# A graph network on one core: Q rows brought into PSUM by a transpose in place of a product with the identity

## The reference

```python
h   = x @ W1 + b1
e   = concatenate([h[dst], h[src] - h[dst]], axis=-1)
m   = relu(e @ W2 + b2)
m   = relu(m @ W3 + b3)
out = relu(segment_max(m, dst, num_segments=N))     # then x = layernorm(x + out)
```

## Time and profile before

| | |
|---|---|
| median of 3 runs | 7734.12 us (7720.88 to 7736.13) |
| profiled execution, its own time | 7735.87 us |
| its span in the trace | 7734.6 us |
| mean granted TensorE clock | 0.794 of full speed |
| PE busy, share of the span | 5133.2 us, 66% |
| PEld | 3121.7 us, 40% |
| DVE | 3723.3 us, 48% |
| ACT | 2423.4 us, 31% |
| POOL | 4559.1 us, 59% |

### The profile page before, as it was taken

The page is one execution under the profiler, slowest core; times in us unless marked ns, Lnnn a source line. Parts: engine busy times, 40 slices in busy tenths (PEclk is TensorE's granted clock), DMA queues, the critical chain, the costliest instruction groups (busy, mean ns, idle before and its releaser), DMA issues.

```text
span 7734.6 us, 94535 instructions
## 1 busy us (share of the span) xinstructions
PE 5133.2 (66%) x25906; PEld 3121.7 (40%) x25906; DVE 3723.3 (48%) x10623; ACT 2423.4 (31%) x7395; POOL 4559.1 (59%) x4719
## 2 busy tenths in 40 slices
PE   3467777777777266767777777725777767767771
PEld 2355555555556133333333333312333333333330
DVE  2222222222223355656666656535665656655664
ACT  1111111111112333333333333323433433333343
POOL 5666666666665655555555555555555555555553
PEclk6787788877788588888888888857888888888885
DMA  4566666666666233333333333313333333333332
GB/s 111 143 183 177 180 182 178 182 180 183 177 182 174 54 85 89 91 88 89 91 90 89 91 85 91 88 48 83 92 89 88 91 84 93 87 89 87 88 92 61
DMA packets 779198, 875.08 MB, mean 113 GB/s; under 512 B 128800, under 2 KB 609525, under 8 KB 778670
## 3 DMA queue, kind: packets, MB, share of 16 engines
q0 software_dynamic: 150304, 304.49, 18.0%
q1 hardware_dynamic: 365790, 354.92, 14.1%
q10 hardware_dynamic: 262576, 209.63, 10.6%
HBM read 536.77 MB, written 331.81 MB: 112 GB/s over the span
## 4 chain that ended last, share of the span: by engine, by line
PE 58%; issue 28%; DVE 4%; another core or an unknown queue 4%; SPq 3%; ACT 2%; POOL 0%; DMA 0%; ACTq 0%; DVEq 0%; POOLq 0%
PE ps L1199 40%; PE ps L1142 5%; PE ps L1132 4%; PE ps L1131 4%; PE ps L1152 3%; SPq L298 1%; SPq L295 1%; DVE ring_b L938 1%; DVE ring_a L892 0%; DVE ring_a L899 0%; POOL ring_a L407 0%; PE ps L1177 0%; ACT x_sb L555 0%; ACT work L509 0%
## 5 line engine op out<-in xcount | busy, mean ns | idle before, releaser
L440 POOL DMA_INDIRECT ring_a<-H_table,src_i x2784 | 2675.5, 961 | 2042.4 <-DVE ring_b L938 1248.4
L1199 PE MATMUL ps<-work,ring_a 128*128 128x390 bf16 x9576 | 1930.8, 359 | 548.0 <-issue 514.4
L1199 PE MATMUL ps<-work,ring_b 128*128 128x390 bf16 x7182 | 1490.6, 345 | 845.9 <-issue 842.0
L380 POOL DMA_INDIRECT ring_a<-Q_table,src_i x1563 | 1513.9, 969 | 827.9 <-issue 455.9
L1199 PEld LDWEIGHTS ps<-work,ring_a 128*128 128x128 bf16 x9576 | 991.1, 105 | 1519.4 <-issue 985.1
L892 DVE TENSOR_TENSOR ring_a<-code,ps 128x896 bf16<-128x896 int16 x1368 | 843.0, 616 | 1279.4 <-remote 1071.9
L590 ACT ACTIVATE code<-src_row,code_bias 128x128 int16<-128x128 int32 x2052 | 636.7, 388 | 2609.5 <-DVE ring_b L892 2562.5
L1199 PEld LDWEIGHTS ps<-work,ring_b 128*128 128x128 bf16 x7182 | 709.3, 100 | 1510.7 <-issue 1091.3
L807 DVE TENSOR_TENSOR_SCAN work<-tab_flat,work,ps 128x512 f32<-128x512 bf16 x390 | 498.8, 1279 | 1607.8 <-remote 1300.7
L938 DVE SCALAR_TENSOR_TENSOR ring_b<-ring_b,gc,ring_a 128x129 f32<-128x129 f32 x3124 | 1092.7, 350 | 138.4 <-issue 66.0
L604 ACT ACTIVATE ring_a<-ring_a,ge 128x129 f32<-128x129 f32 x3126 | 954.9, 390 | 11.4
(11 more groups left out here) (236 smaller groups left out, 2265.8 us busy)
## 6 DMA issues: line engine op xcount, KB each, us to landing
run_sum<-ring_b SPq DMA_DIRECT2D x346, 585.0 KB
work<-P_compact SPq DMA_DIRECT2D x1563, 64.0 KB
tab_flat<-rank_rows ACTq DMA_DIRECT2D x194, 512.0 KB
run_max<-ring_b ACTq DMA_DIRECT2D x194, 512.0 KB
ring_a<-H_table,src_i POOLq DMA_INDIRECT x2784
ring_a<-Q_table,src_i POOLq DMA_INDIRECT x1563
src_row<-in_srcL SPq DMA_DIRECT2D x342, 64.0 KB
H_table<-tab_flat SPq DMA_DIRECT2D x14, 455.0 KB
```

Source lines behind the costliest of these rows:

```text
L380: pool.indirect_dma_start(out=q_ring[:, g % RING, j - j0, :], out_offset=None, in_=Q_table, in_offset=bass.IndirectOffsetOnAxis(ap=srcT_i[ ...
L440: pool.indirect_dma_start(out=h_ring[:, g % RING1, j - j0, :], out_offset=None, in_=H_table, in_offset=bass.IndirectOffsetOnAxis(ap=src_i[ ...
L1199: m = tensor.matmul(ps[at % 2][:, 0:3 * W], lhsT=hot_space[c // 4][:, c % 4, k - k0, :], rhs=split[:, k, :, :].rearrange("p s f -> p (s f) ...
```

## The change

The product of a chunk's Q rows with the identity becomes a transpose: the same operands, the same place in PSUM, still the opening of the accumulation, with TensorE's transpose mode on. Nothing else differs.

```diff
                 for c in range(n):
                     piece = ps[i % 2][:, c * P:(c + 1) * P]
-                    tensor.matmul(piece, lhsT=q_ring[:, g % RING, a + c, :], rhs=ident[:, :], start=True, stop=False)
+                    tensor.matmul(piece, lhsT=q_ring[:, g % RING, a + c, :], rhs=ident[:, :], start=True, stop=False, is_transpose=True)
                     m = tensor.matmul(piece, lhsT=w_ring[:, g % RING, a + c, :], rhs=onto[:, i % 3, c * P:(c + 1) * P],
                                       start=False, stop=True)
                 m.then_inc(placed, 1)
```

## The result

| | before | after |
|---|---|---|
| median | 7727.5 us (7719.82 to 7736.13, 4 runs) | 7794.16 us (7775.93 to 7805.42, 4 runs) |
| ratio | 1 | 1.0078, 95% interval 1.0061 to 1.0095 |
| profiled execution | 7735.87 us | 7805.42 us |

The kernel became slower by 0.8%, 67 us at the medians. The forecast was 7728 us and the range ended at 7765. What came has the sign and nearly the size of rival 2, whose mechanism held in half.

A forecast was written before the change was run, and what follows sets the result against it. The prediction took POOL's beat, not PE's speed, to bound the steady stage. Its sum was 7735.87 − 5.2 − 1.3 = 7729.4 us, on the median's scale 7728 us, with a range of 7670 to 7765.

The forecast's parts named there:

- rival 2: Steady stage: POOL runs 16 gathers without a pause, the beat breaks up, 0.36 us a group lost, +70, about 7800; chance 0.12.
- Steady stage: About 185 groups from 300 to 2400 us: POOL's beat hides PE's saving, so 0 taken, with ends −308 and +70.
- Rival 1: Steady stage: POOL's wait goes, groups of 10.2 us, about 7428, chance 0.08; or shrinks, 7650 to 7710, chance 0.08.
- Tail: From about 2479 us, PE is the path: 47 passes fewer save 5.2 us, a quad taking 2.64 us.
- Start: POOL's first wait, to 262.85 us, ends after PE's first two quads: eight chunks save 1.3 us.
- Rival 3: Tail: the clock falls to half where PE is the path, 5.1 us a quad, +25, about 7755; chance 0.05.
- Rival 4: Line 1131: a transpose that opens an accumulation still goes in two passes, then 7734 us; chance 0.03.

The follow-up runs named there:

- e8_pad: The change with each opening transpose done twice into the same place, 16 passes a quad: 7809.43 us, ratio 1.0000 to the kernel before.
- e10_order: The change with POOL also waiting until the windows of the group four back have landed: 8200.51 us, ratio 1.0515 to the kernel before.
- e17_change: The change unaltered, on an occasion where the kernel before took 6053.96 us: 6058.64 us, ratio 1.0006.
- e18_lean: The change with SP loading window positions without the runtime bounds check, where the kernel before took 6053.96 us: 6063.03 us, ratio 1.0013.

## Why the prediction was wrong

- **Steady stage, "I take 0, the value of every group in rows 6".** This is the step that failed; it came to +67.2 us between the ninth group's start and the last gather. The rows showed that PE's clock could vary its work by 3.2 us without moving the beat, and the step took that as cover for fewer passes too. What the runs showed in its place: with 12 passes POOL runs on for 16 gathers 20 times, each such pair lets out 10.8 of 16 windows, and PE waits 489.7 us for windows where it waited 31.8; with 16 passes (e8_pad) it is 26.4 and the time that of the kernel before, and with the leaner SP the same transpose is faster. The last sentence of the prediction named the hole: PE's pace "by its number of passes and not by its clock". Why POOL finds its signal in time is in part open. The trace of the change has 164 groups that follow one ahead of which POOL had paused. In 47 of them the placing that POOL waits for had ended within the first 6 us of POOL's run, and the 20 times that POOL ran on are all among these. But 27 times it paused all the same, and in the kernel before it paused every time but one (392.75 us), though there 105 of 183 had ended as early. An early placing goes with the running on, then, and is not enough for it.
- **The rivals left SP out.** Windows stand in the prediction once, at the start of the stage. The text ahead of it says that SP issues four groups ahead; in the code that is only the order of its program, its one wait in the loop is for the group six back, as POOL's, and the view of its waits above (4.9 us in 2000) says that it was hardly ever held there. A resource that hardly ever waits, in a stage where PE and POOL do, may be a bound in reserve, and this one view would have pointed at it.
- **Rival 2, +70, "about 7800", at 0.12.** Place, sign and sum came out: it is 72.8 us longer to the first gather of run_max. The price was read from the wrong thing. It took 24.23 us for the pair of groups in the earlier trace rows, 0.73 more than two beats, for every pair of the stage. In the change a pair (10.35 and 12.97) costs nothing, 20 of them came and not 92, and the loss is 3.2 us a time in the group behind, by windows. That the two products agree is chance. Its condition, the second placing signalled before POOL's run is half over, holds for most of the cases: of the 20, the placing had ended within the first 5 us of the run in 15 and by 5.9 us in the other 5. As said above, that isn't enough.
- **Rival 1**, groups of 10.2 us: they came, 20 times (10.2 to 10.4), and were paid back in the next group each time.
- **Tail, −5.2 us.** The price of a quad was right: line 1142 comes at 2583.20 and 2585.82, every 2.62 us, where 2.64 was forecast, so four transposes cost what four passes do. But the tail, from POOL's last gather to the gather of run_max, grew from 33.3 to 37.3 us: PE stood idle once more for a window, for 3.73 us to 2574.91 (its transfer took 5.78 us by the chain of waits), and went on at the half clock for a while.
- **Start, −1.3 us.** POOL's first wait ended at 264.55 us, not before 262.85 but 1.7 after: PE's first placing started at 258.92 where it had started at 257.03, since its windows came later. From there to POOL's start it is 5.63 us, where it was 5.82, 0.2 saved and not 1.3: all eight chunks were placed at a granted clock of 0.50, where the kernel before had the full clock for the second four, as the prediction had assumed.
- **Rival 3, the clock.** From 2580.57 to 2588.12 us, three quads (the last of three chunks) with eight transposes in 18 passes and no gap, the granted clock is 1.00. The rule behind it (the Trainium skill, "TensorE: Matmul & The Clock Gate", Part 4, that transposes don't count as activity in the way of products) did not show itself here. Where the clock was lower, as at 2576.82, where the product of line 1142 took 1.91 us and not 1.02, PE had just waited for a window.
- **Rival 4**, two passes: 1563 passes, so no.

## What to carry to other kernels

Before an engine is made faster, ask which resource of the same stage hardly ever waits, the issuing queue included: SP had 4.4% of the chain of waits before, and it was near the beat. At the 60th group its last window left 8.3 us before PE began to place, at the 144th 41.8, so it gained 33.5 us in 84 groups, 0.4 us a group. When a saving comes out as a loss, look for the group behind the one that moved, and repair the next bound rather than the edit: the same transpose gave +0.8% with one SP program and −0.5% with one that has two instructions fewer a window. The Trainium skill, "DMA: Bandwidth & Descriptors", section "Issuing engines are not separate DMA queues", says that starting transfers from several engines saves only the issuing time, usually small beside the transfer. Here a window's issuing is indeed short beside its 5.15 us of landing, but SP's instructions are 55.7% of the chain, so that time is the thing to save, though no run here moved windows to another queue.

## What the hardware did unexpectedly

Two behaviours, each seen and not explained. First, some five us into a run of POOL's indirect DMAs, and for 2 to 3 us behind its end, SP's register, address and DMA instructions go in steps of 0.70 us and ACT, DVE and POOL get signals late; otherwise most of them take a few hundredths to 0.34 us (the rows at 1029.70 to 1040.27 and those of e10_order). In e10_order POOL's run ends at 1236.44, and SP's steps are short from 1239.52 to about 1254, where POOL has been gathering again since 1249.06. Second, this holds on some occasions and not on others. The waits of DVE's scan in the kernel before, 400 to 2400 us, and in e17_change, on the occasion of 6054 us, 400 to 1900 us:

```profile
DVE work L807 <- remote: 1187.2, 173, 12.6
```

```profile
DVE work L807 <- PE ps L1142: 994.9, 297, 9.0
...
POOL ring_a L380 <- PE ps L1132: 3.0, 10, 0.3
```

In e17_change DVE starts on PE's product by name, POOL waits for PE 3.0 us in 1500, and all its 184 groups take 10.0 to 10.5 us; the change is then within 0.06% of the kernel before (1.0006, interval 0.9997 to 1.0015), and e18_lean 0.13% above it. The whole program is some 1700 us shorter on such an occasion. By the chips' numbers on record it isn't the chip alone: one and the same chip gave 6069 us and, 25 minutes later, 7804 us for the kernel before. A reading of whether this change helps holds only for the occasion on which it was made; what makes a chip behave in the one way or the other isn't known from these runs.
